# The ReLU of attention logits as a maximum on GpSimd, and a masked sum in two halves

## The chip, the cores and the metric

The kernel runs on one core of a Trainium2 chip. The metric is the device time of one execution, in microseconds. The engines are TensorE (PE in the profile), VectorE (DVE), ScalarE (ACT), GpSimd (POOL) and SyncE (SP, which here only issues transfers).

## What is computed

The input is 32 images of 32 channels and 56 x 56 = 3136 positions. Two layers are added to it. The first is a convolution with weights of its own for every position. The second, where nearly all of the time goes, is an attention over the 16 nearest positions, per image:

```python
dist = _pairwise_distance(p)                      # 3136 x 3136 per image
_, nn_idx = jax.lax.top_k(-dist, K)               # K = 16
nbr = pts[bidx, nn_idx]
e, e_n = pts @ W_emb + b_emb, nbr @ W_emb + b_emb
cat = jnp.concatenate([jnp.broadcast_to(e[:, :, None, :], e_n.shape), e_n], axis=-1)
logits = jax.nn.leaky_relu(cat @ W_att + b_att, negative_slope=0.1)
attn = jax.nn.softmax(logits, axis=2)
agg = jnp.sum(nbr * attn, axis=2)
y = jnp.concatenate([pts, agg], axis=-1) @ W_conv + b_conv
```

A logit is leaky_relu(own + other), where `own` belongs to the query and `other` to the neighbour. The kernel doesn't gather neighbours: it works on all 3136 candidates of a query and masks those that are not among the nearest.

## The kernel before

`normalise_input`, `convolve`, `prepare` and `split_halves` run first, `normalise_output` last. Between them stands `attend`, in which the change lies. It takes 128 queries at a time as a tile: 25 tiles (`TILES`) for each of 32 images, 800 in all. Every engine runs its own program over the same sequence of steps (`each_step`), written out for 50 tiles (two images) in a loop. In step s an engine's `body` works on tiles of different age: `tile(-1)` is the coming one, `tile(0)` the one here, `tile(1)` the one before, and so on. Semaphores alone order the engines; each engine's own instructions run in the order in which `body` names them. Where the code says `gate`, the engine waits and then counts that it has passed.

What happens to a tile, in the order of its age:

- TensorE forms the scores (negative distances up to a constant) in two halves of 1568 columns (`score`, L863), and ScalarE copies each half to `scores` (`copy_scores`, L985). The buffer has two places; the first half waits until the masked sum two tiles back has read it.
- VectorE searches the scores in 14 parts of 224 columns with MAX8 (`search`, L1084), seven of them for the coming tile and seven at the head of the next step.
- VectorE merges the 14 x 8 found values (`merge`, L1144): six linked steps that give the 16 best and two bounds, each waiting on the one before through `chain`. The last one signals `doubt_ready`. Where a count made by TensorE from it (`add_doubts`) says that eight per part were too few, `settle_doubts` (L1096) does an exact search over all 3136 columns.
- VectorE turns scores into a bar (`bar`, L1115): min(score - bound, 0), zero for the nearest and hugely negative for all others. For the low 1568 columns (`POOL_COLS`) this is one TENSOR_SCALAR; for the high ones `shares` (0.1 x other) is folded in with one SCALAR_TENSOR_TENSOR. The second signals `barred`.
- ScalarE makes the steep part of the logits (`rise`, L977), Relu(9 x shares + own) over 3136 columns, into `masked`, a ring of five tiles. It waits until TensorE has read the old content (`turned`).
- GpSimd adds `shares` to the low half of it (`add_slope`, L833), in two instructions of 784 columns; the first starts after the previous tile's `barred`, the second after this tile's `doubt_ready`. They signal `logits_ready`.
- VectorE adds the logits and the bar and keeps the row's extreme (`mask`, L1122), one instruction over 3136 columns, a step later. It reads two tensors and signals `masked_ready`.
- ScalarE exponentiates (`exponentiate`, L1000), TensorE transposes in seven groups (`turn`, L884), ScalarE copies these to `turned_sb` (L1017), TensorE multiplies by the images' rows (`aggregate`), VectorE multiplies by the inverse of the sum (`normalise`, L1134) and takes the inverse for a later tile (`invert_total`, L1130).

SyncE loads the next image's tensors (`next_batch`) at the eighth tile of an image.

## Time and profile before

| | |
|---|---|
| time, median of 3 runs | 11978.15 us (11959.74 to 11992.72) |
| span of the profiled execution | 11977.8 us |
| VectorE busy | 10276.0 us (86%) |
| ScalarE busy | 10163.3 us (85%) |
| TensorE busy | 8919.8 us (74%) |
| GpSimd busy | 3199.6 us (27%) |

How to read the rows: "L1127 DVE ... masked<-masked,scores 128x3136 f32" is an instruction of line 1127 on VectorE that writes `masked` from `masked` and `scores`, 128 partitions by 3136 elements. In the timeline a line can stand for several equal instructions in a row; its second number is the time that they span. VectorE starts an instruction before the one ahead has quite ended, so the distance from start to start is what an instruction costs, and it is a little less than its duration. CUSTOM_DVE_ANT_0 is the masked sum with its running minimum. "<-" behind the idle time names who ended it.

### The profile page before, as it was taken

The page shows a single profiled execution, that of the slowest core. Times are in us where ns is not written, and L with a number is a line of the kernel's source. Part 1 is how long each engine was busy: PE and PEld are TensorE (multiplying, and loading weights), DVE is VectorE, ACT ScalarE, POOL GpSimd, SP SyncE. Part 2 cuts the span into 40 slices and gives each one's busy share as a digit, 9 for nine tenths or more (in the row PEclk, how much of TensorE's full clock was granted, in tenths as well). Part 3 has the DMA queues.
Part 4 walks back from the last instruction along what each step waited for, and adds up shares of the span by engine and source line. Part 5 has one row for each costly group of instructions (what it writes and reads, how often), then busy time and mean ns, then how long its engine had stood idle before and what let it go on. Part 6 is the DMA issues. An engine that isn't in the chain of part 4 may idle for free. (4 is left out here: it accounts for less than half of the span.)

```text
span 11977.8 us, 322272 instructions
## 1 busy us (share of the span) xinstructions
PE 8919.8 (74%) x114746; PEld 6368.8 (53%) x114746; DVE 10276.0 (86%) x23897; ACT 10163.3 (85%) x11576; POOL 3199.6 (27%) x2040
## 2 busy tenths in 40 slices
PE   2885667777777777877777777777777777777775
PEld 2664345555555555555555555555555555545553
DVE  1000599999999999999999999999999999999997
ACT  2332489999999999999999998999999999989986
POOL 0221022222222222222222222222222222222221
PEclk9887889999999999999999999999999999999998
DMA  9666800000000000000000000000000000000003
GB/s 164 172 177 175 256 16 17 17 17 16 17 17 17 17 17 16 5 17 17 17 17 16 17 17 16 16 17 16 17 17 4 17 17 17 17 16 16 17 4 132
DMA packets 267542, 480.57 MB, mean 40 GB/s; under 512 B 196964, under 2 KB 197348, under 8 KB 248356
## 3 DMA queue, kind: packets, MB, share of 16 engines
q1 hardware_dynamic: 242532, 349.99, 12.5%
q0 software_dynamic: 23424, 109.21, 2.9%
q8 instruction: 1022, 16.74, 0.6%
q14 instruction: 564, 4.62, 0.1%
HBM read 353.59 MB, written 105.50 MB: 38 GB/s over the span
## 5 line engine op out<-in xcount | busy, mean ns | idle before, releaser
L843 POOL TENSOR_TENSOR masked<-masked,shares_a 128x784 f32<-128x784 f32 x1600 | 2988.8, 1868 | 7371.9 <-DVE rest L1159 4237.3
L1088 DVE MAX8 found<-scores 128x8 f32<-128x224 f32 x11200 | 3479.0, 370 | 223.7 <-ACT scores L990 188.9
L1017 ACT ACTIVATE turned_sb<-psum 128x512 f32<-128x512 f32 (+1 forms) x5600 | 2945.5, 572 | 507.7 <-PE psum L896 431.4
L898 PE MATMUL psum<-ident_a,masked 128*128 128x128 f32 x19200 | 2649.4, 282 | 902.8 <-ACT turned_sb L1017 860.9
L898 PEld LDWEIGHTS psum<-ident_a,masked 128*128 128x128 f32 x19200 | 2373.5, 195 | 1359.9 <-issue 1359.5
L1127 DVE CUSTOM_DVE_ANT_0 masked<-masked,scores 128x3136 f32<-128x3136 f32 x800 | 2719.1, 3399 | 0.2 <-DVE scores L1119 0.2
L990 ACT ACTIVATE scores<-psum 128x1568 f32<-128x1568 f32 x1600 | 2375.1, 1484 | 224.7 <-DVE minus_top L1127 190.0
L1002 ACT ACTIVATE masked<-masked,minus_top 128x3136 f32<-128x3136 f32 x800 | 2363.5, 2954 | 0.0
L982 ACT ACTIVATE masked<-shares_a,own 128x3136 f32<-128x3136 f32 x800 | 2328.4, 2910 | 1.0
L896 PE MATMUL psum<-ident_a,masked 128*128 128x128 f32 (+1 forms) x10400 | 1764.5, 284 | 528.7 <-ACT turned_sb L1017 494.1
L896 PEld LDWEIGHTS psum<-ident_a,masked 128*128 128x128 f32 (+1 forms) x10400 | 1106.7, 139 | 1289.1 <-issue 1213.3
L871 PE MATMUL psum<-points 32*128 32x392 f32 x12800 | 1542.1, 552 | 28.3 <-DMA rows<-table 16.4
L916 PE MATMUL psum<-turned_sb,rows 128*32 128x128 f32 (+1 forms) x40000 | 1554.9, 284 | 0.5 <-ACT inverse_sb L998 0.5
L1119 DVE SCALAR_TENSOR_TENSOR scores<-scores,bound,shares_a 128x1568 f32<-128x1568 f32 x800 | 1467.5, 1834 | 0.0
L916 PEld LDWEIGHTS psum<-turned_sb,rows 128*32 128x32 f32 (+1 forms) x40000 | 1159.1, 113 | 274.0 <-issue 176.5
L295 ACT ACTIVATE w_turned<-w_ps 96x384 f32<-96x384 f32 x784 | 347.2, 486 | 592.0 <-PE w_ps L254 588.4
L882 PE MATMUL psum<-ones,above 128*1 128x1 f32 x1600 | 150.8, 163 | 924.5 <-DVE rest L1159 924.5
L307 DVE COPY conv_sb<-conv_ps 128x128 f32 x196 | 57.1, 291 | 900.9 <-PE conv_ps L276 900.9
L1118 DVE TENSOR_SCALAR scores<-scores,bound 128x1568 f32<-128x1568 f32 x800 | 807.8, 1010 | 8.1 <-DVE bound L1109 2.5
L882 PEld LDWEIGHTS psum<-ones,above 128*1 128x1 f32 x1600 | 84.8, 80 | 1183.3 <-issue 1180.1
L871 PEld LDWEIGHTS psum<-points 32*128 32x128 f32 x12800 | 508.9, 186 | 229.3 <-issue 43.3
L254 PE MATMUL w_ps<-ident_c,w_in 128*96 128x128 f32 x2352 | 398.2, 312 | 232.6 <-DMA w_in<-in_L_conv_weight_dram 204.3
(137 smaller groups left out, 6415.4 us busy)
## 6 DMA issues: line engine op xcount, KB each, us to landing
w_in<-in_L_conv_weight_dram POOLq DMA_DIRECT2D x392, 144.0 KB, 3.4
w_in<-in_L_conv_weight_dram SPq DMA_DIRECT2D x392, 144.0 KB, 3.5
points<-unit SPq DMA_DIRECT2D x128, 392.0 KB
shares_a<-share SPq DMA_DIRECT2D x32, 1568.0 KB
windows<-xg SPq DMA_DIRECT2D x42, 928.0 KB, 13.5
xg<-padded SPq DMA_DIRECT2D x32, 406.0 KB, 16.8
table<-table_sb SPq DMA_DIRECT2D x32, 404.2 KB
rows<-table SPq DMA_DIRECT2D x32, 396.0 KB
```

Of the source, the lines that this page charges most:

```text
L843: nc.gpsimd.tensor_tensor(m, m, shares[:, t.half, k * width:(k + 1) * width], ALU.add).then_inc(logits_ready, 1)
L871: nc.tensor.matmul(ps[:, r * BANK:r * BANK + SCH], points[C * r:C * (r + 1), t.half, t.queries()], points[C * r:C * (r + 1), t.half, at:at ...
L896: last = nc.tensor.transpose(out, block, ident[:])
L898: last = nc.tensor.matmul(out, block, ident[:], start=True, stop=True)
L916: last = nc.tensor.matmul(ps[q:q + C, SUM_BANK:SUM_BANK + P], rows[0:width, t.half, j, 0:C], turned_sb[0:width, t.par, j, :], start=j < PE ...
L982: nc.scalar.activation(masked[:, t.ring, :], shares[:, t.half, :], ACT.Relu, bias=own[:, t.half, at:at + 1], scale=STEEP / SLOPE).then_inc ...
L990: nc.scalar.activation(scores[:, t.par, quad * QUAD:(quad + 1) * QUAD].rearrange("p (a b) -> p a b", b=SCH), ps[:, 0:PER * BANK].rearrange ...
L1002: nc.scalar.activation(masked[:, t.ring, :], masked[:, t.ring, :], ACT.Exp, bias=minus_top[:, t.ring:t.ring + 1], scale=-1.0, accum_out=to ...
L1017: nc.scalar.activation(turned_sb[0:high, t.par, g * GROUP:g * GROUP + width // P, :].rearrange("p a b -> p (a b)"), ps[0:high, bank:bank + ...
L1088: n = step(nc.vector.max(found[:, t.par, c, :], scores[:, t.par, c * PART:(c + 1) * PART]))
L1119: nc.vector.scalar_tensor_tensor(high, high, bound[:, 0:1], shares[:, t.half, POOL_COLS:N], ALU.subtract, ALU.min).then_inc(barred, 1)
L1127: nc.vector.tensor_tensor_reduce(m, m, scores[:, t.par, :], -1.0, -NEVER, ALU.add, ALU.min, minus_top[:, t.ring:t.ring + 1]).then_inc(mask ...
```

## The change

- `rise` on ScalarE goes. Relu(9 x shares + own) + bar is rewritten as max(9 x shares, -own), which differs from the Relu by a constant of the row, and the softmax doesn't see that. ScalarE makes `minus_own` in place of `own` (`begin_batch`, moved behind the second `copy_scores`).
- GpSimd makes `steep` = 9 x shares once for each image (`steepen`), and for each tile max(min(steep, 3e38), minus_own) over 3136 columns into `masked` (`clamp`). Then it adds `shares` on the low 1568 columns, now in one instruction. Both are done for the coming tile. GpSimd waits for `turned` in ScalarE's place, and no longer for `barred` or `doubt_ready`.
- `mask` becomes `mask_low` and `mask_high`, 1568 columns each; the second starts its running minimum from the first's (`low_top`). The first copy of the scores waits for the low one only, the second for the high one.
- `merge` is taken apart. VectorE's `body` puts other work between its steps: the high half, `normalise`, `invert_total` and the coming tile's searches.

The diff, without declarations:

```diff
-            def add_slope(t, passed):
-                pool.wait_ge(rises_ready, t.count(1, 1))
-                if passed is not None:
-                    pool.wait_ge(barred, passed.count(1, 1))
-                width = POOL_COLS // 2
-                for k in range(2):
-                    if k == 1:
-                        pool.wait_ge(doubt_ready, t.count(1, 1))
-                    m = masked[:, t.ring, k * width:(k + 1) * width]
-                    nc.gpsimd.tensor_tensor(m, m, shares[:, t.half, k * width:(k + 1) * width], ALU.add).then_inc(logits_ready, 1)
+            def steepen(t):
+                gate(pool, batch_in[t.half], t.pair(16 * LOADS, 16 * LOADS), pool_passed)
+                if not (isinstance(t.i, int) and t.at == 0):
+                    gate(pool, logits_ready, t.count(), pool_passed)
+                nc.gpsimd.tensor_scalar(steep[:], shares[:, t.half, :], 1.0, STEEP / SLOPE,
+                                        ALU.mult, ALU.mult).then_inc(steep_ready, 1)
+            def clamp(t, used):
+                gate(pool, steep_ready, t.batch(1, 1), pool_passed)
+                gate(pool, own_ready, t.batch(2, 2), pool_passed)
+                if used is not None:
+                    gate(pool, turned, used.count(T_GROUPS, T_GROUPS), pool_passed)
+                at = t.c if t.c < TILES - 1 else OWN
+                nc.gpsimd.tensor_scalar(masked[:, t.ring, :], steep[:], -NEVER, minus_own[:, t.half, at:at + 1],
+                                        ALU.min, ALU.max).then_inc(clamped, 1)
+            def add_slope(t):
+                pool.wait_ge(clamped, t.count(1, 1))
+                m = masked[:, t.ring, 0:POOL_COLS]
+                nc.gpsimd.tensor_tensor(m, m, shares[:, t.half, 0:POOL_COLS], ALU.add).then_inc(logits_ready, 1)
             def body(tile):
-                if tile(0):
-                    add_slope(tile(0), tile(1))
+                coming = tile(-1)
+                if coming:
+                    if coming.c == 0:
+                        steepen(coming)
+                    clamp(coming, tile(RING - 1))
+                    add_slope(coming)
...
             act.wait_ge(bias_made, 1)
-            nc.scalar.activation(att_bias[:], ps[:, 0:1], ACT.Copy, scale=STEEP).then_inc(bias_ready, 1)
...
                 act.wait_ge(bias_ready, 1)
                 act.wait_ge(batch_in[t.half], t.pair(16 * LOADS, 16 * LOADS))
-                nc.scalar.activation(own[:, t.half, 0:TILES - 1], rows[:, t.half, 0:TILES - 1, C], ACT.Identity,
-                                     bias=att_bias[:, 0:1]).then_inc(own_ready, 1)
-                nc.scalar.activation(own[:, t.half, TILES:TILES + 1], rows[:, t.half, TILES:TILES + 1, C], ACT.Identity,
-                                     bias=att_bias[:, 0:1]).then_inc(own_ready, 1)
-                act.wait_ge(own_ready, t.batch(2, 2))
-            def rise(t, used):
-                if used is not None:
-                    act.wait_ge(turned, used.count(T_GROUPS, T_GROUPS))
-                at = t.c if t.c < TILES - 1 else OWN
-                nc.scalar.activation(masked[:, t.ring, :], shares[:, t.half, :], ACT.Relu, bias=own[:, t.half, at:at + 1],
-                                     scale=STEEP / SLOPE).then_inc(rises_ready, 1)
+                if not (isinstance(t.i, int) and t.at == 0):
+                    act.wait_ge(logits_ready, t.batch(TILES))
+                nc.scalar.activation(minus_own[:, t.half, 0:TILES - 1], rows[:, t.half, 0:TILES - 1, C], ACT.Identity,
+                                     bias=att_bias[:, 0:1], scale=-1.0).then_inc(own_ready, 1)
+                nc.scalar.activation(minus_own[:, t.half, TILES:TILES + 1], rows[:, t.half, TILES:TILES + 1, C], ACT.Identity,
+                                     bias=att_bias[:, 0:1], scale=-1.0).then_inc(own_ready, 1)
             def copy_scores(t, quad, used):
                 act.wait_ge(scored, t.count(SCORED, SCORED_FREE + PER * (quad + 1)))
                 if used is not None:
-                    act.wait_ge(masked_ready, used.count(1, MASKED_FREE + 1))
+                    if quad == 0:
+                        act.wait_ge(low_masked, used.count(1, 1))
+                    else:
+                        act.wait_ge(masked_ready, used.count(1, MASKED_FREE + 1))
                 nc.scalar.activation(scores[:, t.par, quad * QUAD:(quad + 1) * QUAD].rearrange("p (a b) -> p a b", b=SCH),
                                      ps[:, 0:PER * BANK].rearrange("p (a b) -> p a b", b=BANK)[:, :, 0:SCH],
...
@@ -1027,15 +1043,14 @@
                     copy_turned(past, 0, tile(5))
                 if coming:
                     copy_scores(coming, 0, tile(1))
-                    if coming.c == 0:
-                        begin_batch(coming)
-                    rise(coming, tile(RING - 1))
                 if past:
                     copy_turned(past, 1)
                 if older:
                     copy_inverse(older, tile(SUM_LAG + 1))
                 if coming:
-                    copy_scores(coming, 1, None)
+                    copy_scores(coming, 1, tile(1))
+                    if coming.c == 0:
+                        begin_batch(coming)
                 if past:
                     copy_turned(past, 2)
                     copy_turned(past, 3)
@@ -1115,17 +1130,24 @@
             def bar(t):
                 low, high = scores[:, t.par, 0:POOL_COLS], scores[:, t.par, POOL_COLS:N]
-                step(nc.vector.tensor_scalar(low, low, bound[:, 0:1], 0.0, ALU.subtract, ALU.min))
+                nc.vector.tensor_scalar(low, low, bound[:, 0:1], 0.0, ALU.subtract, ALU.min).then_inc(barred, 1)
                 nc.vector.scalar_tensor_tensor(high, high, bound[:, 0:1], shares[:, t.half, POOL_COLS:N],
                                                ALU.subtract, ALU.min).then_inc(barred, 1)
-            def mask(t):
-                gate(dve, logits_ready, t.count(2, 2), dve_passed)
-                gate(dve, barred, t.count(1, 1), dve_passed)
-                m = masked[:, t.ring, :]
-                nc.vector.tensor_tensor_reduce(m, m, scores[:, t.par, :], -1.0, -NEVER, ALU.add, ALU.min,
-                                               minus_top[:, t.ring:t.ring + 1]).then_inc(masked_ready, 1)
+            def mask_low(t):
+                gate(dve, logits_ready, t.count(1, 1), dve_passed)
+                gate(dve, barred, t.count(2, 2), dve_passed)
+                m = masked[:, t.ring, 0:POOL_COLS]
+                nc.vector.tensor_tensor_reduce(m, m, scores[:, t.par, 0:POOL_COLS], -1.0, -NEVER, ALU.add, ALU.min,
+                                               low_top[:, t.par:t.par + 1]).then_inc(low_masked, 1)
+            def mask_high(t):
+                gate(dve, low_masked, t.count(1, 1), dve_passed)
+                m = masked[:, t.ring, POOL_COLS:N]
+                nc.vector.tensor_tensor_reduce(m, m, scores[:, t.par, POOL_COLS:N], -1.0, low_top[:, t.par:t.par + 1],
+                                               ALU.add, ALU.min, minus_top[:, t.ring:t.ring + 1]).then_inc(masked_ready, 1)
             def invert_total(t):
                 dve.wait_ge(exp_ready, t.count(1, 1))
@@ -1141,22 +1163,40 @@
                 nc.vector.tensor_tensor(agg[:, t.group_par, at:at + P], ps[:, SUM_BANK:SUM_BANK + P], inverse_sb[:],
                                         ALU.mult).then_inc(agg_ready, 1)
-            def merge(t, n):
-                found_all = found[:, t.par, :, :].rearrange("p a b -> p (a b)")
-                last = best[:, NEIGHBOURS - 1:NEIGHBOURS]
+            last = best[:, NEIGHBOURS - 1:NEIGHBOURS]
+            def found_of(t):
+                return found[:, t.par, :, :].rearrange("p a b -> p (a b)")
...
+            def top_first(t, n):
                 dve.wait_ge(chain, n)
-                n = step(nc.vector.max(best[:, 0:H8], found_all))
+                return step(nc.vector.max(best[:, 0:H8], found_of(t)))
...
+                nc.vector.scalar_tensor_tensor(rest[:], found_of(t), bound[:, 1:2], weight8[:].rearrange("p a b -> p (a b)"),
                                                ALU.is_ge, ALU.mult, accum_out=above[:, 0:1]).then_inc(doubt_ready, 1)
             def body(tile):
@@ -1164,19 +1204,35 @@
                 if here:
                     n = search(here, 1)
                 if tile(1):
-                    mask(tile(1))
+                    mask_low(tile(1))
                 if here:
-                    merge(here, n)
+                    n = top_first(here, n)
+                if tile(1):
+                    mask_high(tile(1))
+                if here:
+                    n = drop_first(here, n)
                 if tile(NORM_LAG):
                     normalise(tile(NORM_LAG))
+                if here:
+                    n = top_second(n)
                 if tile(3):
                     invert_total(tile(3))
+                if here:
+                    n = lower_bound(n)
                 if coming:
-                    search(coming, 0, 0, 2)
+                    search(coming, 0, 0, 1)
+                if here:
+                    n = set_bound(here, n)
+                if coming:
+                    search(coming, 0, 1, 2)
+                if here:
+                    count_above(here, n)
+                if coming:
+                    search(coming, 0, 2, 4)
                 if here:
                     ask_doubts(here)
                 if coming:
-                    search(coming, 0, 2)
+                    search(coming, 0, 4)
                 if here:
                     settle_doubts(here)
                     bar(here)
```

## Rows read from the trace of the kernel before

**Rows 1.** The page: span, busy shares by engine, tenths in 40 slices
```profile
span 11977.8 us, 322272 instructions
...
PE 8919.8 (74%) x114746; PEld 6368.8 (53%) x114746; DVE 10276.0 (86%) x23897; ACT 10163.3 (85%) x11576; POOL 3199.6 (27%) x2040
...
DVE  1000599999999999999999999999999999999997
ACT  2332489999999999999999998999999999989986
```

**Rows 2.** One line's view, L1127: duration min/median/max ns, first and last start
```profile
...
L1127 DVE CUSTOM_DVE_ANT_0 masked<-masked,scores x800: 3393/3398/3426, 1517.9 to 11839.2; 128x3136 f32<-128x3136 f32 x160
```

**Rows 3.** Busy us of each engine in one stretch, instructions in brackets
```profile
...
6000.00:8000.00 2000.00, 1554.29 (x18087) 1099.36 (x18083) 1922.85 (x4520) 1872.85 (x2078) 580.97 (x311) 0.97 0.07 16
```

**Rows 4.** Timeline: start us, us, engine, line, operation; VectorE and ScalarE
```profile
...
7006.09 1.83 DVE L1119 SCALAR_TENSOR_TENSOR scores<-scores,bound,shares_a 128x1568 f32<-128x1568 f32 x1
7007.86 2.13 DVE L1088 MAX8 found<-scores 128x8 f32<-128x224 f32 x7
7009.92 3.39 DVE L1127 CUSTOM_DVE_ANT_0 masked<-masked,scores 128x3136 f32<-128x3136 f32 x1
...
7013.25 0.26 DVE L1149 MAX8 best<-found 128x8 f32<-128x112 f32 x1
7013.55 0.09 DVE L1151 MATCH_VALUE_LOAD rest<-best,found 128x8 f32 x1
...
7015.01 0.08 DVE L1159 DVE_READ_ACCUMULATOR rest<-found,bound,weight 128x1 f32 x1
7015.17 0.29 DVE L1141 TENSOR_TENSOR agg<-psum,inverse_sb 128x128 f32<-128x128 f32 x1
...
7017.56 1.00 DVE L1118 TENSOR_SCALAR scores<-scores,bound 128x1568 f32<-128x1568 f32 x1
...
7022.32 3.39 DVE L1127 CUSTOM_DVE_ANT_0 masked<-masked,scores 128x3136 f32<-128x3136 f32 x1
...
7006.01 1.50 ACT L990 ACTIVATE scores<-psum 128x1568 f32<-128x1568 f32 x1
...
7008.32 2.96 ACT L1002 ACTIVATE masked<-masked,minus_top 128x3136 f32<-128x3136 f32 x1
...
7020.82 2.96 ACT L1002 ACTIVATE masked<-masked,minus_top 128x3136 f32<-128x3136 f32 x1
```

**Rows 5.** Groups by line: count, busy us, mean ns, idle before and releasers
```profile
...
L1088 DVE MAX8 found<-scores 128x8 f32<-128x224 f32 x11200 | 3479.0, 370 | 223.7 <-ACT scores L990 188.9 <-issue 25.3
L843 POOL TENSOR_TENSOR masked<-masked,shares_a 128x784 f32<-128x784 f32 x1600 | 2988.8, 1868 | 7371.9 <-DVE rest L1159 4237.3 <-DVE scores L1119 3104.7 <-ACT masked L982 29.9
...
L982 ACT ACTIVATE masked<-shares_a,own 128x3136 f32<-128x3136 f32 x800 | 2328.4, 2910 | 1.0
...
L1119 DVE SCALAR_TENSOR_TENSOR scores<-scores,bound,shares_a 128x1568 f32<-128x1568 f32 x800 | 1467.5, 1834 | 0.0
...
L1104 DVE MAX8 best<-scores 128x8 f32<-128x3136 f32 x15 | 51.4, 3428 | 0.5
...
L1108 DVE TENSOR_SCALAR scores<-scores 128x3136 f32<-128x3136 f32 x15 | 26.9, 1793 | 0.5
```

**Rows 6.** Groups on GpSimd outside the loop, same columns
```profile
...
L830 POOL TENSOR_SCALAR_AFFINE_SELECT ident_a<-ident_a 128x128 f32<-128x128 f32 x1 | 0.3, 287 | 72.6 <-DVE own_feat L1059 72.6
...
L235 POOL MEMSET ident_c<- 128x128 f32 x1 | 0.2, 204 | 67.8 <-POOLq L44 67.8
...
L1333 POOL MEMSET const-float32-1.0<- 128x1 f32 x1 | 0.1, 98 | 0.0
```

**Rows 7.** Timeline of GpSimd, same window
```profile
...
7008.07 1.88 POOL L843 TENSOR_TENSOR masked<-masked,shares_a 128x784 f32<-128x784 f32 x1 [3.56 <-DVE scores L1119]
7015.17 1.87 POOL L843 TENSOR_TENSOR masked<-masked,shares_a 128x784 f32<-128x784 f32 x1 [5.21 <-DVE rest L1159]
```

**Rows 8.** Timeline of TensorE, same window: the last transpose group
```profile
...
7012.00 0.27 PE L896 MATMUL psum<-ident_a,masked 128*64 128x128 f32 x1 [0.45 <-ACT turned_sb L1017]
```

24 lines of the change are left out of this document (17 added, 7 removed).

## The prediction

> **What bounds the kernel now.** I read the page first, to see which engines are full in which part of the span [rows 1]. VectorE and ScalarE stand at nine tenths (ScalarE at eight now and then) from the sixth slice on; GpSimd is busy for 27% of the span. So one stage, `attend`, is the kernel: from the first masked sum (L1127) at 1517.9 us to the last at 11839.2 us [rows 2] there are 799 intervals, 12.92 us each. What lies around them is 11977.8 - 10321.3 = 1656 us, which the change doesn't touch. The profiled execution (11977.8 us) is at the median of the runs, so I sum against it.
>
> Then I ask which of the two full engines sets the 12.92 us. The windows view gives VectorE 96% and ScalarE 94% of a late stretch [rows 3]: too close to tell. The timeline of one tile does tell. One VectorE round is 7009.92 to 7022.32, 12.40 us, and in it VectorE has one gap, at the normalise step (7015.01 to 7015.17; at other places the operation behind an accumulator read starts with it, as at 7013.25, so about 0.16 us is waiting) [rows 4]. VectorE's own loop is thus about 12.2 us, and ScalarE's, from one exponential at 7008.32 to the next at 7020.82, 12.5 us. The two are nearly balanced. The rest of the mean is the 15 exact searches, each three passes like L1104's 3.43 us and one of 1.79 us (L1108), 12.1 us: 180 us in all [rows 5].
>
> **ScalarE's part of the change.** It loses the rise, 800 times 2.91 us (L982) [rows 5]. Its loop falls from 12.5 to about 9.6 us and it is no longer a bound. Alone, this is worth only what separates the two loops, because VectorE's 12.2 us stands right behind it: 0.3 us a tile, 240 us. The copy of the first half of the scores now waits for the low half of the masked sum, which ends about 1.8 us sooner than the whole one; the second copy waits for the high half. The exponential, and the turned copies behind these, are queued there, and ScalarE has 2.6 us of air to absorb it. `begin_batch` (two small activations, 32 times) moves behind the second copy; only the batch's first clamp waits for it, and its sum is wanted a whole tile later. I cost it at nothing.
>
> **VectorE's part.** The masked sum in two halves: L1127 takes 3.33 us from start to start (7009.92 to 7013.25) [rows 4]; a two-tensor operation on 1568 columns takes 1.77 us (L1119, 7006.09 to 7007.86) [rows 4], so two cost 3.54: plus 0.2 us. The merge: each of its steps waits for the one before (7013.25 to 7013.55 is 0.30 us for an operation of 0.26) [rows 4], while unlinked MAX8 of 0.37 us start every 0.30 us [rows 4, 5]. Other work between two linked steps hides some 0.03 us of wait and 0.065 us of drain, 0.095 us at each of five places: minus 0.5 us. VectorE's own loop becomes 12.2 + 0.2 - 0.5 = 11.9 us. The bar's two operations are as before. The masked sum's logits are made a whole tile ahead, so its gate costs nothing as long as GpSimd keeps up.
>
> **GpSimd's part.** Now it adds `shares` on 2 x 784 columns, 1.868 us each, 3.7 us a tile [rows 5]; after, one instruction on 1568, again about 3.7 us. New is the clamp, one tensor and one output on 3136 columns, for which this trace has no row. From below: a memset takes 204 ns for 128 columns and 98 for one, 0.82 ns a column, 2.7 us for 3136. From above: the two-tensor add, 2.26 ns a column after the same fixed 0.1 us, 7.2 us. Nearest in kind is the affine select, 287 ns for 128 columns, 1.5 ns a column after the fixed part, 4.8 us; but it also forms an index [rows 6]. I take the middle between memset and select, 3.7 us. `steepen` is one more such pass in 25 tiles, 0.15 us a tile. GpSimd's sum of 7.4 us (6.4 to 10.9) fits in 11.9: by its own work it is no bound.
>
> **What the two do side by side** decides the case. Before, GpSimd waits before each half for `barred` or `doubt_ready`, which carry no data that it reads. Its two instructions lie at 7008.07 to 7009.95 and 7015.17 to 7017.04 [rows 7], in both cases beside MAX8, which read one tensor; the masked sum begins at 7009.92 and the bar at 7017.56, when they are over or within 30 ns of it [rows 4]. That is the pattern of all 800 tiles: the waits that release GpSimd are the bar's end and the merge's end [rows 5]. MAX8 isn't slowed (0.37 us throughout). But a masked sum reads two tensors at 1.08 ns a column, as fast as MAX8 reads one, and L1118 runs at 0.64 ns a column (1.00 us for 1568), so these use an access that MAX8 doesn't. Whether GpSimd needs that same access no row shows. Two ends: nothing, or they take turns. I take turns as the value: MAX8 being left alone says only that the first access is free, and the clamp's 3.7 us with the add's 3.7 us can't stay in the MAX8 stretches once the waits are gone. By this the change is priced so. Let T be the end of the high half.
> - VectorE: in the trace the bar starts 4.31 us after the masked sum's end (7013.25 to 7017.56) [rows 4]; less the 0.16 us gap, the first merge step (0.3) and four hidden links (0.4), the bar starts at T+3.45, ends at T+6.15, and seven MAX8 end at T+8.2.
> - The clamp waits for `turned` of the sixth group: from the second scores copy to that transpose's end is 7006.01 to 7012.27, 6.3 us [rows 4, 8], and 0.2 us for each wake: clamp at T+6.65, end T+10.35. The low half, due at T+8.2, waits 2.15 us and ends at T+12.1.
> - The add has waited since the clamp's end, goes next and ends at T+15.8; the high half waits for it and ends at T+17.6.
>
> A round of 17.6 us. 799 x 17.6 + 1656 + 180 + some 100 for `steepen` = 16,000 us. With the clamp at its ends: 15,100 and 18,800. If the order settles so that both GpSimd instructions start with a MAX8 stretch (2.06 us at the round's head, about 1.9 us before the bar), the round is 11.9 + 1.6 + 1.8 = 15.3 us, 14,200; with the cheapest clamp 13,400.
>
> The Trainium skill has a rule on this (SBUF — State Buffer, section "SBUF: two separate sides"): the port pair that VectorE and GpSimd share is "an exclusive lock, not a bandwidth split", taken for a whole instruction, by a VectorE operation in a two-port mode or with two SBUF inputs, or by a GpSimd one. The row of MAX8 beside GpSimd agrees with it, but the clash itself is in no row of this trace. By that rule the sum is the 16,000 above, by the MAX8 row extended to everything it is the first rival's.
>
> **Rivals.**
> 1. No clash: VectorE's round is 11.9 us, GpSimd's 7.4 us beside it. 799 x 11.9 + 1656 + 180 = 11,350 us, 5% faster; 11,250 to 11,700 with the links worth less. For it: MAX8 unslowed, and masked sums that begin 30 ns before GpSimd's reported end aren't longer (3.40 us) [rows 4, 5]. Against it: that overlap may be nothing but how ends are reported.
> 2. GpSimd yields: it is held while VectorE runs the halves and the bar, and VectorE keeps its pace. These take 3.54 + 2.70 = 6.2 us a tile, so GpSimd needs 6.2 + 7.4 = 13.6 us a round and the masked sum waits for its logits: 799 x 13.6 + 1656 + 180 + 50 = 12,750 us; 11,950 to 15,550 over the clamp's ends. If both only slow each other a little, the loss lies in between; one of 0.6 to 0.9 us a tile, which eats the gain, gives no change.
> 3. The clamp alone is dear: above 8.2 us it makes GpSimd's loop longer than 11.9 us whatever the clash, and the add is late for the masked sum. At 5 ns a column it would be 15.7 + 3.7 = 19.4 us a round, 17,350 us. Nothing in the trace shows a pass so slow.
> 4. The change frees nothing, if ScalarE still waits: not likely, as the copies' condition comes sooner.
>
> **How the numbers follow.** A run tells 0.3% from no change here. Turns: 0.69, GpSimd yields 0.10, dear clamp 0.02: slower 0.81. No clash: 0.16 faster. No change: 0.03. The likeliest gives 16,000. Its own range is 13,400 to 18,800; to hold 8 in 10 the range must take in most of the second rival too: 12,300 to 18,800.
>
> **What would show it.** Turns: masked sums and bar with idle VectorE time or longer durations just where a GpSimd instruction runs, MAX8 unchanged, VectorE's round above 15 us, ScalarE waiting long for the low half, GpSimd instructions stretched where they start beside the bar. No clash: L1127's halves at 1.8 us each beside a running clamp. Wrong most of all if the clamp costs other than 2.7 to 7.2 us, or if GpSimd is the one that is held back: then its instructions grow, VectorE's keep their lengths, and VectorE's idle time stands before the low half, put down to GpSimd's add.

## The result

The changed kernel takes 16,893 us (median of 4 runs, 16,880 to 16,897) against 11,979 us: 1.410 times as long, interval 1.408 to 1.412. The forecast was slower, 16,000 us, in 12,300 to 18,800. The page of the kernel after, for [rows 1]:

```profile
span 16894.8 us, 327185 instructions
...
PE 11135.8 (66%) x114746; PEld 7892.5 (47%) x114746; DVE 14330.1 (85%) x25497; ACT 8178.3 (48%) x10776; POOL 5748.4 (34%) x2072
...
DVE  1016999999999999999999999999999999999997
ACT  2334454545445545455455544554554545545544
...
PEclk9877777777777777777777777777777777777777
```

ScalarE has fallen from nine tenths to four or five, and VectorE is as full as before. The granted TensorE clock is at seven tenths of full speed (0.755 on the mean over the span, where the kernel before had 0.952). From one merge to the next it is 19.08 us on the mean, against 12.92. The groups by line (count, busy us, mean ns, idle before), for [rows 5]:

```profile
L1103 DVE MAX8 found<-scores 128x8 f32<-128x224 f32 x11200 | 3638.7, 376 | 1012.3 <-ACT scores L1006 1012.2
...
L860 POOL TENSOR_TENSOR masked<-masked,shares_a 128x1568 f32<-128x1568 f32 x800 | 2851.4, 3564 | 66.8
L853 POOL TENSOR_SCALAR masked<-steep,minus_own 128x3136 f32<-128x3136 f32 x800 | 2597.3, 3247 | 9630.2 <-PE psum L917 8982.6 <-ACT minus_own L996 627.0 <-PE psum L919 20.7
L1194 DVE SCALAR_TENSOR_TENSOR bound<-under,best,bound_low 128x2 f32<-128x2 f32 x800 | 2512.7, 3141 | 0.0
...
L1189 DVE SCALAR_TENSOR_TENSOR bound_low<-over,best,margin 128x2 f32<-128x2 f32 x800 | 1644.0, 2055 | 0.1
```

The two bound steps of the merge, L1189 and L1194, work on 2 columns. They took 0.22 us each; now they take 2.06 and 3.14 us. Nothing else that VectorE runs in every round has grown like that. (The one-tensor pass of the 15 exact searches, L1123 now, has: 3.34 us on the mean for 1.79, 3136 columns.) The timeline of one round shows beside what they stand (start us, us). VectorE:

```profile
9002.21 0.09 DVE L1179 MATCH_VALUE_LOAD rest<-best,found 128x8 f32 x1
...
9002.95 2.47 DVE L1189 SCALAR_TENSOR_TENSOR bound_low<-over,best,margin 128x2 f32<-128x2 f32 x1
9005.34 0.38 DVE L1103 MAX8 found<-scores 128x8 f32<-128x224 f32 x1
9005.65 3.34 DVE L1194 SCALAR_TENSOR_TENSOR bound<-under,best,bound_low 128x2 f32<-128x2 f32 x1
...
9015.36 2.15 DVE L1103 MAX8 found<-scores 128x8 f32<-128x224 f32 x7 [1.16 <-ACT scores L1006]
```

GpSimd and ScalarE in the same round:

```profile
9002.54 2.87 POOL L853 TENSOR_SCALAR masked<-steep,minus_own 128x3136 f32<-128x3136 f32 x1 [12.53 <-PE psum L917]
9005.49 3.48 POOL L860 TENSOR_TENSOR masked<-masked,shares_a 128x1568 f32<-128x1568 f32 x1
```

```profile
9013.74 1.48 ACT L1006 ACTIVATE scores<-psum 128x1568 f32<-128x1568 f32 x1 [1.83 <-PE psum L896]
...
9020.40 0.27 ACT L1033 ACTIVATE turned_sb<-psum 64x128 f32<-64x128 f32 x1 [0.35 <-PE psum L917]
```

The clamp runs from 9002.54 to 9005.41, and the first bound step, begun at 9002.95, ends at 9005.42. The add runs from 9005.49 to 9008.97, and the second bound step, begun at 9005.65, ends at 9008.99. The MAX8 between them, which starts 0.15 us ahead of the add and runs on beside it, takes its 0.38 us. At 9015.36 VectorE has waited 1.16 us for the scores, which ScalarE copies from 9013.74 on.

Where the 4,915 us went, from the two tables of groups (sums over 800 tiles): bound steps 1644 + 2513 - 353 = 3,804 us longer; the masked sum in halves (L1142, L1149) 1573 + 1458 - 2719 = 312; VectorE's wait for scores 1012 - 189 = 823; a new idle time ahead of the bar 260; bar and count some 155. That is 5,354 us. The 440 us by which this is too much, 0.55 us a tile, I put down to what the merge lost in waits and drains when other work came between its steps. It is a remainder of durations that overlap at their ends, not measured by itself; but in `dve_only` below, where nothing is held, the same terms come to 427 us too much, 0.53 us a tile.

### The profile page after: what moved, and what is told of

It reads as the page before. It is cut to its first block and busy times, and to the rows that moved or that the text cites. A ratio compares the mean times of both kernels' runs of the same rounds, so it can differ in the third digit from the quotient of the medians.

```text
span 16894.8 us, 327185 instructions
## 1 busy us (share of the span) xinstructions
PE 11135.8 (66%) x114746; PEld 7892.5 (47%) x114746; DVE 14330.1 (85%) x25497; ACT 8178.3 (48%) x10776; POOL 5748.4 (34%) x2072
## 5 line engine op out<-in xcount | busy, mean ns | idle before, releaser
L853 POOL TENSOR_SCALAR masked<-steep,minus_own 128x3136 f32<-128x3136 f32 x800 | 2597.3, 3247 | 9630.2 <-PE psum L917 8982.6
L919 PE MATMUL psum<-ident_a,masked 128*128 128x128 f32 x19200 | 3359.0, 330 | 53.5 <-issue 42.5
L919 PEld LDWEIGHTS psum<-ident_a,masked 128*128 128x128 f32 x19200 | 2945.3, 235 | 941.5 <-issue 932.0
L860 POOL TENSOR_TENSOR masked<-masked,shares_a 128x1568 f32<-128x1568 f32 x800 | 2851.4, 3564 | 66.8
L1194 DVE SCALAR_TENSOR_TENSOR bound<-under,best,bound_low 128x2 f32<-128x2 f32 x800 | 2512.7, 3141 | 0.0
L892 PE MATMUL psum<-points 32*128 32x392 f32 x12800 | 2114.3, 741 | 24.4 <-DMA rows<-table 15.9
L937 PE MATMUL psum<-turned_sb,rows 128*32 128x128 f32 (+1 forms) x40000 | 1943.7, 340 | 0.5 <-ACT inverse_sb L1014 0.5
L1189 DVE SCALAR_TENSOR_TENSOR bound_low<-over,best,margin 128x2 f32<-128x2 f32 x800 | 1644.0, 2055 | 0.1
L1149 DVE CUSTOM_DVE_ANT_0 masked<-masked,scores,low_top 128x1568 f32<-128x1568 f32 x800 | 1573.0, 1966 | 0.2 <-DVE low_top L1142 0.2
L1142 DVE CUSTOM_DVE_ANT_0 masked<-masked,scores 128x1568 f32<-128x1568 f32 x800 | 1458.1, 1823 | 0.2 <-DVE scores L1134 0.2
```

The costliest lines, as they stand in the source:

```text
L853: nc.gpsimd.tensor_scalar(masked[:, t.ring, :], steep[:], -NEVER, minus_own[:, t.half, at:at + 1], ALU.min, ALU.max).then_inc(clamped, 1)
L860: nc.gpsimd.tensor_tensor(m, m, shares[:, t.half, 0:POOL_COLS], ALU.add).then_inc(logits_ready, 1)
L892: nc.tensor.matmul(ps[:, r * BANK:r * BANK + SCH], points[C * r:C * (r + 1), t.half, t.queries()], points[C * r:C * (r + 1), t.half, at:at ...
L919: last = nc.tensor.matmul(out, block, ident[:], start=True, stop=True)
L937: last = nc.tensor.matmul(ps[q:q + C, SUM_BANK:SUM_BANK + P], rows[0:width, t.half, j, 0:C], turned_sb[0:width, t.par, j, :], start=j < PE ...
L1189: return step(nc.vector.scalar_tensor_tensor(bound_low[:], over[:], last, margin[:], ALU.mult, ALU.subtract))
```

## The experiments

**Pairs by themselves.** A stretch ahead of `attend` in the kernel before, `probe`, in which GpSimd runs one operation and VectorE a MAX8 and one other beside it:

```diff
     split_halves(nc, half_sq, pieces)
+    probe(nc)
...
+    # in probe, on VectorE, for each GpSimd operation and each VectorE operation:
+        dve.sem_inc(go, 1)
+        nc.vector.max(small[:], a[:, 0:512]).then_inc(ddone, 1)
+        nc.vector.scalar_tensor_tensor(c[:, 0:2], a[:, 0:2], 1.5, b[:, 0:2], ...)   # or one of seven others
```

> The kernel before, with a stretch of its own ahead of attend that measures pairs. GpSimd runs nothing, then the clamp on 3136 columns, then a memset of 3136, then the two-tensor add on 1568; beside each, VectorE runs one MAX8 of 512 and then one of eight operations: a two-tensor step of 2 columns, one-tensor steps of 1, 2 and 512 columns, a two-tensor add of 512, one of PSUM and one tensor, a second MAX8, a one-tensor step that writes PSUM. Theory A (they take turns, for a whole instruction): with nothing beside them all take 0.2 to 0.6 us; beside the clamp (2.9 us) and the add (3.5 us) the two-tensor operations end only when GpSimd's does, so the 2-column one shows 2 us or more, and the 512-column one-tensor step, at 0.6 ns a column, does too; MAX8 and the ones with PSUM stay as they are. Theory B (the access is shared in small portions): the 2-column step stays at 0.22 us, and only the 512-column ones grow, in proportion, to at most twice their time. At the end, a 256-column clamp (0.3 us) asked for while VectorE runs 3136 columns: by A it shows 2 us or more, by B under 0.6. The memset reads nothing, so A leaves open whether it holds a two-tensor step; the one-tensor 512-column step should wait for it by A. The whole kernel: 11980 us plus 150 to 250.

```profile
1492.72 2.87 POOL L1332 TENSOR_SCALAR pr_pb<-pr_pa,pr_col 128x3136 f32<-128x3136 f32 x1 [95.98 <-DVEq L1352]
1493.19 2.41 DVE L1355 SCALAR_TENSOR_TENSOR pr_c<-pr_a,pr_b 128x2 f32<-128x2 f32 x1
...
1496.39 0.13 DVE L1357 TENSOR_SCALAR pr_c<-pr_a 128x1 f32<-128x1 f32 x1
...
1499.41 2.30 DVE L1359 TENSOR_SCALAR pr_c<-pr_a 128x2 f32<-128x2 f32 x1
```

Here the clamp on 3136 columns runs each time (2.87 us), and it starts some 0.5 us ahead of VectorE's operation. Durations in us, alone and beside each GpSimd operation:

| VectorE operation | alone | clamp | memset | add of two |
|---|---|---|---|---|
| two tensors, 2 columns | 0.14 | 2.41 | 0.14 | 2.89 |
| two tensors, 512 | 0.67 | 2.81 | 0.67 | 3.41 |
| one tensor, 1 column | 0.14 | 0.13 | 0.13 | 0.13 |
| one tensor, 2 columns | 0.15 | 2.30 | 2.09 | 2.89 |
| one tensor, 512 | 0.41 | 2.55 | 2.35 | 3.15 |
| one tensor and PSUM, 512 | 0.67 | 0.67 | 0.67 | 0.67 |
| one tensor to PSUM, 512 | 0.68 | 0.67 | 0.68 | 0.68 |
| MAX8, 512 | 0.68 | 0.68 | 0.68 | 0.67 |

Theory A stands in every cell that it spoke of, and B fails in every cell where the two differ: an operation either runs as alone or ends only when GpSimd's has ended, and 2 columns are enough for it to be held. The one-tensor form that is held is the faster one (0.41 us for 512 columns, where the others take 0.67), on 512 columns and on 2, but not on 1. The memset, which reads nothing, holds these and not the two-tensor ones. The other way round, at the end of the stretch:

```profile
1574.57 1.79 DVE L1380 TENSOR_SCALAR pr_c<-pr_a 128x3136 f32<-128x3136 f32 x1 [0.48 <-POOL pr_pb L1342]
1574.58 2.13 POOL L1342 TENSOR_SCALAR pr_pb<-pr_pa,pr_col 128x256 f32<-128x256 f32 x1
```

A clamp of 256 columns, 0.3 us of work by the rate above, was started with an operation of VectorE's of 1.79 us and took 2.13 us; another one, started with an add of two tensors of 3.42 us, took 3.75. So VectorE's operation holds GpSimd's in the same way. The whole run took 12,078 us, 94 more than before, where I had expected 150 to 250.

The Trainium skill (SBUF — State Buffer, "SBUF: two separate sides") states just this: an exclusive lock for the whole instruction, taken by two-port modes and by two SBUF inputs, the latter only against a GpSimd operation that reads SBUF. The table agrees with it, the memset's column too.

**A memset in the clamp's place**, so that the ReLU part of the logits is left out:

```diff
-                nc.gpsimd.tensor_scalar(masked[:, t.ring, :], steep[:], -NEVER, minus_own[...], ALU.min, ALU.max).then_inc(clamped, 1)
+                nc.gpsimd.memset(masked[:, t.ring, :], 0.0).then_inc(clamped, 1)
```

> The changed kernel with a memset of the same 3136 columns in the clamp's place (2.6 us by the memset's rate, for 2.87), so the ReLU part of the logits is left out; all waits stay. If it is GpSimd's reading that holds a two-tensor VectorE operation, the lower bound (L1189, 2.06 us on the mean) falls to 0.22 us, and only what meets the add stays long: a round of 19.06 us loses 1.8 us or so, 15,300 to 15,700 us. If any GpSimd instruction holds it, L1189 keeps about 1.8 us and the time stays at 16,600 to 16,900 us.

```profile
L1102 DVE MAX8 found<-scores 128x8 f32<-128x224 f32 x11200 | 3648.5, 377 | 1849.3 <-ACT scores L1005 1849.3
...
L1193 DVE SCALAR_TENSOR_TENSOR bound<-under,best,bound_low 128x2 f32<-128x2 f32 x800 | 2407.8, 3010 | 0.0
...
L1188 DVE SCALAR_TENSOR_TENSOR bound_low<-over,best,margin 128x2 f32<-128x2 f32 x800 | 182.6, 228 | 0.1
```

And in one round:

```profile
9006.79 2.71 POOL L853 MEMSET masked<- 128x3136 f32 x1 [11.17 <-PE psum L916]
```

```profile
9008.57 0.22 DVE L1188 SCALAR_TENSOR_TENSOR bound_low<-over,best,margin 128x2 f32<-128x2 f32 x1
```

The first bound step is back at 0.23 us, and it runs inside a GpSimd instruction of nearly the same length (2.71 us for 2.87), so it is GpSimd's reading that holds a two-tensor step. But the time is 16,195 us, not 15,300 to 15,700: of the 1.83 us that it gives back, 1.05 come again as a wait for scores (1849 us, for 1012). So the time of a held step isn't simply added to the round.

**The bound steps with one tensor**, nothing left out:

```diff
-                return step(nc.vector.scalar_tensor_tensor(bound_low[:], over[:], last, margin[:], ALU.mult, ALU.subtract))
+                for k in range(2):
+                    n = step(nc.vector.tensor_scalar(bound_low[:, k:k + 1], last, 1.0 + (k + 1) * TINY, (k + 1) * MARGIN, ...))
+                return n   # and the second bound step alike
```

> The changed kernel with the two 2-column bound steps made as two 1-column steps each, of one tensor with constants, so that neither reads a second tensor from SBUF; nothing is left out. Theory A: these four steps take under 0.25 us each, though GpSimd's clamp and add run beside them just as before; the stall moves to the next two-tensor operation, the count (L1199 before) and is shorter by the single-tensor work that now fits in front, about 1 us: GpSimd's two instructions are 6.4 us and VectorE has some 2 us beside them. Time 15,300 to 16,400 us. A rival (small linked steps are held whatever they read, by their wait or their write): they stay at 2 and 3 us, and the time at 16,900 or above.

```profile
L1149 DVE CUSTOM_DVE_ANT_0 masked<-masked,scores,low_top 128x1568 f32<-128x1568 f32 x800 | 1988.2, 2485 | 0.6 <-issue 0.4 <-DVE low_top L1142 0.2
...
L1133 DVE TENSOR_SCALAR scores<-scores,bound 128x1568 f32<-128x1568 f32 x800 | 1298.5, 1623 | 261.3 <-DVEq L1126 258.8 <-DVE bound L1124 2.5
...
L1203 DVE SCALAR_TENSOR_TENSOR rest<-found,bound,weight 128x112 f32<-128x112 f32 x800 | 1226.5, 1533 | 0.0
```

15,198 us, 10% less, slightly under what was expected. The steps take 0.15 to 0.20 us beside the same clamp and add, and the hold moves on: to the count (1.53 us for 0.33), the bar's low part (1.62 for 1.01) and the high half (2.49 for 1.85). So a small linked step isn't held for being one. But this run changes two things together, from two tensors to one and from 2 columns to 1, and in the probe a one-tensor step of 2 columns was held too (2.30 us). Which of the two freed it here isn't shown: no run has a two-tensor step of 1 column.

**TensorE's order:**

```diff
-                if here:
-                    add_doubts(here)
 ...
                 if coming:
                     score(coming, 1)
+                if here:
+                    add_doubts(here)
```

> The changed kernel with one TensorE step moved: the doubt count (L903) behind the second half of the coming tile's scores in place of ahead of it. Theory: VectorE's wait for scores (L1103, 1.27 us a tile) comes from that half being queued on TensorE behind the count, which waits for the held merge; with the order changed this wait falls below 0.3 us and the round from 19.06 us to about 18, 15,900 to 16,200 us, while the two held bound steps stay as long as they are. Rival: the scores are late because TensorE runs at a granted clock of 0.755; then the wait and the time stay within 2%.

```profile
L1103 DVE MAX8 found<-scores 128x8 f32<-128x224 f32 x11200 | 3632.5, 375 | 88.2 <-ACT scores L1006 81.0 <-issue 6.9
...
L1149 DVE CUSTOM_DVE_ANT_0 masked<-masked,scores,low_top 128x1568 f32<-128x1568 f32 x800 | 2665.2, 3331 | 0.2 <-DVE low_top L1142 0.2
...
L1189 DVE SCALAR_TENSOR_TENSOR bound_low<-over,best,margin 128x2 f32<-128x2 f32 x800 | 1843.6, 2305 | 0.1
...
L1194 DVE SCALAR_TENSOR_TENSOR bound<-under,best,bound_low 128x2 f32<-128x2 f32 x800 | 1022.6, 1278 | 0.0
```

15,702 us, a little more gained than expected. The wait for scores is gone (81 us, for 1012): it had come from the second half of the scores being queued on TensorE behind the doubt count, which waited for the held merge. The bound steps didn't stay as they were: the second is held less (1.28 us), the first a little more (2.31 us), the high half more (3.33 us). GpSimd's start has moved: in the round at 9010 us the clamp begins 1.3 us ahead of the high half's end; in two rounds of the changed kernel it began 0.3 us behind that end (9002.54) and 0.6 us ahead of it (9020.58). The clock alone was not the cause, but it seems to have a part, whose size no run measures. Windows of the changed kernel's round (PE, PEld, DVE, ACT and POOL busy us; then the granted clock):

```profile
9000.00:9004.00 4.00, 3.89 (x35) 2.75 (x33) 4.00 (x11) 2.70 (x7) 1.46 (x1) 1.00 0.00 0
9004.00:9009.80 5.80, 0.00 (x0) 0.00 (x0) 5.80 (x8) 1.33 (x2) 4.89 (x2) 0.66 0.00 0
9009.80:9015.40 5.60, 5.51 (x28) 3.82 (x28) 4.14 (x9) 1.94 (x3) 0.00 (x0) 0.50 0.00 0
9015.40:9022.00 6.60, 6.60 (x89) 5.03 (x89) 6.60 (x18) 5.98 (x9) 1.42 (x1) 0.95 0.01 2
```

While the merge is held, TensorE has nothing to do for 5.8 us. After that it works for 5.6 us at a granted clock of 0.50, the lower of its two levels (1.2 GHz), and the scores that all wait for lie in it: the same eight matmuls take 1.69 us there and 0.94 at the full clock.

**GpSimd's part alone:** the whole masked sum and the linked merge as before.

> The changed kernel with VectorE's part undone: the whole masked sum and the linked merge as before, the clamp and the add on GpSimd without their old waits. If the loss comes from GpSimd's instructions lying beside VectorE's two-tensor ones, it is here nearly whole: 15,500 to 17,500 us, and held again are whichever two-tensor operations follow the masked sum (the bounds, 0.22 us before) or the masked sum itself. If taking the merge apart and halving the sum were a part of the loss, this one is well under 15,000.

16,292 us, 88% of the loss. Again the two bound steps are the held ones (1.96 and 3.20 us on the mean); the masked sum is at 3.46 us.

**The same work behind two waits:**

```diff
+                if passed is not None:
+                    gate(pool, barred, passed.count(2, 2), pool_passed)       # ahead of the clamp
...
+                if here is not None:
+                    gate(pool, doubt_ready, here.count(1, 1), pool_passed)    # ahead of the add
```

> The changed kernel with two more waits on GpSimd and nothing else: the clamp waits for the previous tile's bar, the add for this tile's count, so that they start where only MAX8 run. The same work in other places. By turns: the clamp (2.87 us, 0.2 us after the bar) ends 1.0 us behind seven MAX8 (2.06 us) and holds the low half by that; the add (3.48 us) holds the bar by about 2 us; the bound steps are back at 0.22 us. A round of 11.9 + 1.0 + 2.0 + 0.3 = 15.2 us, 14,000 us, within 13,500 to 14,500. If what costs is GpSimd's amount of work and not its place, the time stays above 16,000.

```profile
L1137 DVE TENSOR_SCALAR scores<-scores,bound 128x1568 f32<-128x1568 f32 x800 | 2088.2, 2610 | 255.7 <-DVEq L1130 253.3 <-DVE bound L1128 2.4
...
L1193 DVE SCALAR_TENSOR_TENSOR bound_low<-over,best,margin 128x2 f32<-128x2 f32 x800 | 1300.7, 1626 | 0.1
```

What GpSimd waited for in the same run (us in total, times, longest us):

```profile
POOL masked L855 <- PE psum L921: 5227.1, 719, 12.9
```

14,765 us, 2,128 less with no work taken away, so the place decides. It is 265 us above the range, for the clamp mostly didn't land where I meant it to: what released it was still the transpose (719 times), later than the bar, and it held the first bound step (1.63 us). The add holds the bar's low part by 1.6 us (2.61 us for 1.01), where I had expected about 2. The second bound step is free (0.20 us).

**VectorE's part alone:** the masked sum in halves and the merge taken apart, ScalarE's rise and GpSimd's adds as before.

> The kernel before with VectorE's part of the change alone: the masked sum in two halves and the merge taken apart; the rise stays on ScalarE and GpSimd's two adds of 784 columns keep their waits, for the bar's end and the merge's last step. My theory prices VectorE's own loop at 12.2 + 0.2 - 0.5 = 11.9 us, but ScalarE's loop of 12.5 us then stands alone, so a round falls from 12.9 to 12.6 or 12.7: 11,700 to 11,900 us. The second add (1.87 us) now meets the bar, as only five MAX8 are left behind the count: up to 0.3 us. Rival: this part brings nothing or costs something, 11,980 to 12,150, if the links' cost doesn't go away or the second add holds the bar longer.

12,812 us, 1.070 times the kernel before (1.068 to 1.072). I had priced this part as a gain. VectorE's timeline, then TensorE's:

```profile
8002.72 0.22 DVE L1179 SCALAR_TENSOR_TENSOR bound_low<-over,best,margin 128x2 f32<-128x2 f32 x1
8003.55 0.40 DVE L1093 MAX8 found<-scores 128x8 f32<-128x224 f32 x1 [0.61 <-ACT scores L995]
...
8004.29 0.32 DVE L1189 SCALAR_TENSOR_TENSOR rest<-found,bound,weight 128x112 f32<-128x112 f32 x1
...
8006.47 1.04 DVE L1123 TENSOR_SCALAR scores<-scores,bound 128x1568 f32<-128x1568 f32 x1 [0.29 <-DVEq L1116]
...
8010.43 2.15 DVE L1093 MAX8 found<-scores 128x8 f32<-128x224 f32 x7 [1.17 <-ACT scores L995]
```

```profile
8004.91 0.19 PE L884 MATMUL psum<-ones,above 128*1 128x1 f32 x2 [2.69 <-DVE rest L1189]
...
8006.60 1.69 PE L873 MATMUL psum<-points 32*128 32x392 f32 x8
```

The first MAX8 of the coming tile now stands between the bound steps, and it waits 0.61 us for ScalarE's copy. The second bound step and the count stand behind it; TensorE, idle for 2.69 us, then works at the lower clock; and the head of the next round waits 1.17 us for scores. A second loss stands ahead of the bar, 0.29 us here and 256 us in all. The bar waits until the count's answer (`doubts`, written at 8005.14) has been read, which took 1.33 us here; only three MAX8 are left to fill that time, where the kernel before had five. Two runs take this apart. In `dve_tight` the coming tile's MAX8 go back behind the count:

```diff
-                if coming:
-                    search(coming, 0, 0, 1)
                 if here:
                     n = set_bound(here, n)
-                if coming:
-                    search(coming, 0, 1, 2)
-                if here:
                     count_above(here, n)
                 if coming:
-                    search(coming, 0, 2, 4)
+                    search(coming, 0, 0, 2)
                 if here:
                     ask_doubts(here)
                 if coming:
-                    search(coming, 0, 4)
+                    search(coming, 0, 2)
```

> VectorE's part of the change alone (12,812 us, 7% slower than before), with one thing undone: the coming tile's MAX8 no longer stand between the two bound steps and the count, but behind the count, as before. Theory C: they cost that much there because each waits for scores that ScalarE hasn't copied yet (0.6 and 1.0 us in that run's timeline), which holds the count behind them, and with it TensorE's queue (the doubt count, then the second half of the coming scores) and so the head of the next round. Then the round falls by 1.0 us or more, VectorE's wait for scores falls from 1014 us to under 400, and the time is 11,850 to 12,150 us. Rival D: it is the half-and-half masked sum with its copies' new conditions that costs; then the time stays above 12,500.

12,033 us, 1.005 (1.003 to 1.006): theory C holds, and that one order was 780 of the 832 us lost. Not all of it is the wait for scores: VectorE's idle time ahead of its MAX8 falls from 1,020 to 403 us, and that ahead of the bar from 256 to 6, as five MAX8 stand there again. What is left of VectorE's part gains nothing and loses a little. In `dve_pe` the order on VectorE stays and TensorE's is the one of `pe_order`:

> VectorE's part alone again (12,812 us), VectorE's order as in the change, but TensorE makes the second half of the coming tile's scores ahead of the doubt count. Theory C says that the 1.17 us at the head of a round come from that queue and go, while the wait of the first MAX8 inside the merge stays (0.6 to 1.0 us): 12,000 to 12,400 us, and TensorE's granted clock nearer to that of before (0.95). If the count's place in the queue doesn't matter, the time stays within 1% of 12,812.

12,272 us, 1.025 (1.023 to 1.026), in the range: TensorE's order gives back 540 of the 832 us. VectorE's wait for scores is 220 us in all, so the one inside the merge did not stay at 0.6 to 1.0 us a tile. In its place VectorE waits 258 us for the doubt count, which now stands behind the scores on TensorE, and the 256 us ahead of the bar are still there. The granted clock was 0.900 and not near 0.95.

**Three attempts at a kernel that beats both.** `fit_a` is `dve_tight` with one-tensor bound steps and three pieces for GpSimd, each released where VectorE reads one tensor; one is the ReLU of the high half:

```diff
+                nc.gpsimd.tensor_scalar(masked[:, t.ring, POOL_COLS:N], steep[:, t.half, :], own[:, t.half, at:at + 1], 0.0,
+                                        ALU.add, ALU.max).then_inc(high_ready, 1)
```

> VectorE's part of the change, and of GpSimd's part only what fits beside one-tensor operations of VectorE: behind the bar the ReLU of the high 1568 columns as max(steep + own, 0), 1.45 us; behind the masked sum an add on 480 columns, 1.1 us; behind the count an add on 800, 1.8 us. The bound steps are 1-column steps of one tensor; the bar folds in shares from column 1280 on (0.15 us more). ScalarE makes the ReLU of the low half only, 1.45 us less. If turns are all there is: no VectorE operation is held by more than 0.1 us, its loop is about 12.0 us, ScalarE's 11.1, and the time 799 x 12.1 + 1656 + 180 = 11,500 us, 11,350 to 11,700, faster than before by 2 to 5%. Rival: three starts of GpSimd a tile don't land in their gaps, two-tensor operations are held, and it is 11,980 or above.

```profile
L848 POOL TENSOR_SCALAR masked<-steep,own 128x1568 f32<-128x1568 f32 x800 | 4445.1, 5556 | 2870.1 <-DVE scores L1146 2490.0 <-PE psum L918 351.1 <-ACT own L997 29.0
...
L1154 DVE CUSTOM_DVE_ANT_0 masked<-masked,scores 128x1568 f32<-128x1568 f32 x800 | 2847.8, 3560 | 0.2 <-DVE scores L1146 0.2
```

13,744 us, 1.148 (1.146 to 1.150). The adds fitted their places, but this form took 5.56 us for 1568 columns, 3.5 ns a column, where the clamp's took 0.9, and it held the low half (3.56 us for 1.77). What in the form costs this is open. In `fit_b` the piece has the clamp's form, on columns 1200 to 3136, and VectorE's masked sum is whole; the normalise step and the inverse stand inside the merge:

```diff
+                nc.gpsimd.tensor_scalar(masked[:, t.ring, POOL_COLS:N], steep[:], -NEVER, minus_own[:, t.half, at:at + 1], ALU.min, ALU.max)
...
-                step(nc.vector.tensor_scalar(low, low, bound[:, 0:1], 0.0, ALU.subtract, ALU.min))
+                step(nc.vector.tensor_scalar(low, low, bound[:, 0:1], minus_own[:, t.half, at:at + 1], ALU.subtract, ALU.min))
```

> A kernel meant to beat both, from the one before: VectorE's masked sum whole; the normalise step and the inverse inside the merge, ahead of the bounds; the bound steps as before. GpSimd has three pieces a tile, each behind a wait for a place where VectorE reads one tensor: behind the bar the clamp in the form min by a constant, max by a column (0.9 ns a column in the changed kernel; the form add a column, max a constant took 3.5 in fit_a) on columns 1200 to 3136, 1.8 us; behind the masked sum the add on 400 columns, 0.95 us; behind the count the add on 800, 1.85 us. ScalarE makes the ReLU on 1200 columns only (1.8 us less a tile), VectorE's bar subtracts own on these so that both parts differ from the ReLU by the same constant. VectorE's loop by my sum 12.2 - 0.2 + 0.2 = 12.2 us, ScalarE's 10.7, so a round of 12.25 us in place of 12.7 and 11,620 us, 11,500 to 11,800, 1.5 to 4% faster. If a two-tensor operation is held in one of the three places it shows there, and the time is 11,980 or above.

The timeline of one round, GpSimd, then VectorE:

```profile
8004.92 1.87 POOL L846 TENSOR_SCALAR masked<-steep,minus_own 128x1936 f32<-128x1936 f32 x1 [3.34 <-DVE scores L1146]
8010.29 1.03 POOL L859 TENSOR_TENSOR masked<-masked,shares_a 128x400 f32<-128x400 f32 x1 [3.50 <-DVE minus_top L1155]
8012.05 1.88 POOL L859 TENSOR_TENSOR masked<-masked,shares_a 128x800 f32<-128x800 f32 x1 [0.73 <-DVE rest L1191]
```

```profile
8014.04 0.88 DVE L1145 TENSOR_SCALAR scores<-scores,bound,minus_own 128x1200 f32<-128x1200 f32 x1
8014.85 2.22 DVE L1146 SCALAR_TENSOR_TENSOR scores<-scores,bound,shares_a 128x1936 f32<-128x1936 f32 x1
```

12,180 us, 1.017 (1.016 to 1.019). Here the clamp and the larger add end with or before the MAX8 beside them, and the smaller add lengthens the first bound step by 0.05 us (0.27 us for 0.22). What was wrong is the sum for VectorE: its undisturbed round is 12.35 us, not 12.2. Against the 12.40 of the kernel before, the merge gives back 0.35 (1.85 us from its first step to the MAX8 behind it, for 2.20, the gap of 0.16 in it), but 368 columns more of the bar fold in `shares`, which costs 0.25 (bar 0.80 + 2.15 us, for 0.93 + 1.77). Other rounds are longer, with scores that come late behind matmuls at the lower clock: eight of them take 1.69 us from 8013.63, for 0.94 from 8006.33. TensorE had paused for 2.12 us ahead of the former; but it had paused for 2.20 us a round earlier too and kept the full rate, so the pause alone doesn't tell. `fit_c` moves the second half of the scores ahead of a transpose group and the inverse, on TensorE and ScalarE:

> fit_b (12,180 us, 1.7% slower than before) with one order changed: TensorE makes the second half of the coming tile's scores right behind the doubt count, ahead of a transpose group and of the spread of the inverse, and ScalarE copies it ahead of the inverse. In fit_b no VectorE operation was held by GpSimd, and an undisturbed round took 12.35 us; others were 0.3 to 1.1 us longer because the scores came late, behind matrix work that ran at the lower clock (1.69 us for 0.94) after TensorE had been idle for 2 us. If that is all that is in the way, VectorE's wait for scores falls from 377 to under 100 us and the time is 799 x 12.4 + 1656 + 180 = 11,750 us, 11,680 to 11,880: 1 to 2.5% faster than before. If the late scores have another cause (the masked sum's end, which frees the buffer), the time stays above 12,050.

12,034 us, 1.004 (1.003 to 1.006), outside the 11,680 to 11,880 that I had expected. The wait for scores falls from 377 to 234 us, not below 100, and the granted clock is 0.892. The order was a part of it; what makes the rest late stays open. No version beat the kernel before.

## Why the prediction was right, point by point

**Right: GpSimd's new instructions and VectorE's two-access operations take turns, for whole instructions.** The probe shows it pair by pair, and `gated` that the same work costs 2,128 us less elsewhere. The trace of before had no row of such a pair [rows 4, 7], so 0.69 for this end of the bound was a judgement. It came out as one would read the waits on `barred` and `doubt_ready`: they carry no data, and without them GpSimd lands beside two-tensor operations.

**Wrong in place: which operations are held.** I let the clamp meet the low half and the add the high half, and counted the bound steps as hidden small work inside T+3.45. In truth these two, 2 columns wide, met both instructions in nearly every round. The step that failed is the clamp's start. Its last part is right: from the second scores copy to the transpose's end it is 13.74 to 20.40, 6.7 us, for 6.3. But I let that copy start at T+0.2, and it starts 11.5 us after T (T is 9002.21, at the match load; the copy is at 9013.74), because the scores behind it wait on TensorE for the doubt count, which waits for the merge. I followed the wait through ScalarE's queue and not through TensorE's. The trace of before could have told me:

```profile
7015.39 0.19 PE L882 MATMUL psum<-ones,above 128*1 128x1 f32 x2 [0.92 <-DVE rest L1159]
```

```profile
7018.51 1.50 ACT L990 ACTIVATE scores<-psum 128x1568 f32<-128x1568 f32 x1
```

There too the second half's scores follow the doubt count on TensorE (from 7016.41 to 7017.52), and their copy starts 5.3 us behind the masked sum's end (7013.25), not 0.2.

**Terms of the sum.** The clamp took 2.87 us unheld, where I took 3.7 (bounds 2.7 to 7.2); by the memset's rate it would have been 2.7, so the nearest row was the lower bound's [rows 6]. The add took 3.48 us for 3.7. VectorE's own loop, the round above less what is held or idle, is 18.96 - 2.25 - 3.12 - 0.30 - 1.16 = 12.1 us, for 11.9. Held time was 3,804 us by the bound steps, 4.8 us a tile, where I had 2.15 + 3.5 = 5.65. So the 16,000 rests on a dear clamp and too long a hold, made good by what I had not seen: the wait for scores (823 us) and the idle time ahead of the bar (260 us). That it came within 6% is in part luck. The mean round was 19.1 us, for 17.6. The clamp's two ends, added up with `steepen` at the same rate, give 15,200 and 18,900, for the 15,100 and 18,800 that I wrote.

**Not shown: what ScalarE's relief is worth.** ScalarE went from 94% busy to about half, and the time did not follow; it was no bound any more, as the prediction had it. But no run relieves it alone, so the 240 us that I gave this stay untested. In `fit_b` and `fit_c`, where it is relieved without a clash, VectorE's own work changed too, and its undisturbed round was 12.35 us in `fit_b`.

**Wrong: VectorE's part as a gain of 0.3 us a tile.** Alone it cost 832 us, 1.04 us a tile. The two terms that I had priced came about as I said: the halves 181 us in `dve_only` for 160, and the merge's links by the remainder 0.53 us a tile for 0.5. The step that failed is the filler: I priced MAX8 between linked steps by the drain they hide, and put at nothing what they cost elsewhere. That was their own wait for scores (1,014 us in `dve_only`, for 189) and the idle time ahead of the bar that they no longer fill (256 us, for 8). `dve_tight` gives 780 us of the 832 back by moving them.

**The rivals.** No clash is refuted by the probe. GpSimd yielding is half true: it is held too (the clamp's mean is 3.25 us for 2.87), since who starts first goes first. A dear clamp didn't occur, but `fit_a` met a form that dear (3.5 ns a column would be 11 us for 3136, above the 8.2 of the third rival). That the probe's rule is the cause in the full kernel rests on `memset`, `bounds_one` and `gated` together. What a microsecond less of holding gave back varied: summed over the bound steps, the count, the bar and the halves, `memset` took 1,585 us less and gained 699 (0.44), `bounds_one` took 1,949 less and gained 1,696 (0.87).

## What to carry to other kernels

Before work goes to GpSimd, list what VectorE runs beside it. In the runs here, operations with two SBUF tensors waited for the whole GpSimd instruction if that one reads, even with 2 columns; one-tensor operations in the faster form waited for the memset too. MAX8, a one-tensor step of 1 column, and operations with one SBUF tensor and PSUM on the other side did not. In this kernel the small steps of a serial chain were the worst ones to expose, for TensorE's queue stood behind them. When an independent operation is used to fill the gap between two linked steps, ask what it waits for itself, and which time it filled where it stood before.

## What the runs showed that I had not expected

- One column and two differ: a one-tensor step of 1 column took 0.13 us beside the clamp, the memset and the add, one of 2 columns 2.30 us beside the clamp.
- GpSimd's time for one tensor with two scalars depends on the form: min by a constant and max by a column took 2.87 us for 3136 columns (0.9 ns a column), two multiplications by constants 2.80 us, add of a column and max by a constant 5.56 us for 1568 (3.5 ns).
- After a pause of 5.8 us TensorE was at 0.50 for the next 5.6 us, though it was busy throughout, and back at 0.95 in the stretch behind. In `dve_only` a pause of 2.7 us was followed by 5.5 us at 0.50.
